# Four-head attention and a graph network on one core: scores by 32-row tiles of TensorE, row sums by VectorE

## The reference

```python
x = _layernorm(x + _L0_gnn_ref(x, adj, ...))   # two graph convolutions, then LSTMs over windows of 1 to 4 nodes
x = _layernorm(x + _L1_gnn_ref(x, W, adj))     # attention, 4 heads of 32 features, masked by adj == 0
x = _layernorm(x + _L2_gnn_ref(x, adj, ...))   # aggregation by the normalized adjacency, two layers, two batch norms
x = _layernorm(x + _L3_gnn_ref(x, W, adj, bias))
```

```python
qkv = h @ W
scores = jnp.einsum("bhid,bhjd->bhij", q, k) / np.sqrt(HEAD_DIM) + mask
attn = jax.nn.softmax(scores, axis=-1)
out = jnp.einsum("bhij,bhjd->bhid", attn, v)
...
agg = jnp.einsum('nm,bmd->bnd', A_hat, features)
h = jax.nn.relu(_batchnorm(x @ W1.T + b1, g1, be1))   # needs the mean and variance over all batches first
```

## Time and profile before

| what | value |
|---|---|
| median of three runs | 1684.76 us (1682.45 to 1689.03) |
| the profiled execution's own time | 1689.47 us |
| its span in the profile | 1687.7 us |
| mean granted TensorE clock | 0.962 |
| busy: PE, DVE, ACT, POOL | 90%, 75%, 62%, 24% |
| stretch of the LSTM block | 0 to 803 us |
| stretch of attention | 803 to 1364 us |
| both later stretches | 1364 to 1688 us |

### The profile page before, as it was taken

How to read it: one execution, slowest core, us unless ns; L and a number is a source line. 1 busy time by engine, 2 the same in 40 slices (tenths; PEclk the granted TensorE clock), 3 DMA queues, 4 the chain that set the end, 5 groups by cost and what they waited for, 6 DMA issues and landing times.

```text
span 1687.7 us, 28097 instructions
## 1 busy us (share of the span) xinstructions
PE 1514.9 (90%) x9014; PEld 1208.4 (72%) x9076; DVE 1263.0 (75%) x2989; ACT 1042.9 (62%) x1984; POOL 407.1 (24%) x641
## 2 busy tenths in 40 slices
PE   3999999899989989995699999999999879899997
PEld 3888888787888888895477767677777645555554
DVE  3578767677776777777688888888888745577775
ACT  2666576566656666664466666666666436557776
POOL 2122212112121221221233233323333300023332
PEclk9999999999999999998799999999999979989999
DMA  3000000000000000000000000000000000022221
GB/s 95 1 1 24 15 1 13 14 13 14 1 26 13 1 13 14 13 1 15 1 20 14 19 12 19 19 12 19 12 19 12 19 19 0 0 70 87 87 87 57
DMA packets 19519, 37.62 MB, mean 22 GB/s; under 512 B 3313, under 2 KB 4849, under 8 KB 19313
## 3 DMA queue, kind: packets, MB, share of 16 engines
q1 hardware_dynamic: 18576, 34.49, 6.4%
q10 hardware_dynamic: 864, 2.11, 0.3%
HBM read 19.81 MB, written 16.78 MB: 22 GB/s over the span
## 4 chain that ended last, share of the span: by engine, by line
PE 61%; DVE 18%; ACT 12%; issue 5%; POOL 2%; DMA 1%; ACTq 0%; DVEq 0%; POOLq 0%
PE banks L391 14%; PE banks L393 13%; PE banks L392 13%; PE banks L1497 5%; PE banks L1504 5%; ACT early_scratch L796 4%; PE banks L1464 3%; DVE x_all L506 3%; ACT attention_scratch L750 2%; ACT attention_rounded L750 2%; PE banks L1414 2%; DVE early_scratch L985 2%; PE banks L1424 2%; DVE consts L464 1%; DVE attention_rounded L1035 1%
## 5 line engine op out<-in xcount | busy, mean ns | idle before, releaser
L391 PE MATMUL banks<-early_rounded 128*128 128x128 f32 (+3 forms) x1424 | 458.4, 322 | 64.9 <-DVE early_rounded L990 31.1
L392 PE MATMUL banks<-early_rounded 128*128 128x128 f32 (+3 forms) x1424 | 454.8, 319 | 0.0
L393 PE MATMUL banks<-early_rounded 128*128 128x128 f32 (+3 forms) x1424 | 454.4, 319 | 0.0
L796 ACT ACTIVATE early_scratch<-banks,consts 128x256 f32<-128x256 f32 (+2 forms) x624 | 311.7, 565 | 133.4 <-PE banks L393 119.3
L391 PEld LDWEIGHTS banks<-early_rounded 128*128 128x128 f32 x1424 | 280.3, 197 | 90.3 <-issue 42.0
L392 PEld LDWEIGHTS banks<-early_rounded 128*128 128x128 f32 x1424 | 280.1, 197 | 14.7
L393 PEld LDWEIGHTS banks<-early_rounded 128*128 128x128 f32 x1424 | 280.2, 197 | 14.0
L660 POOL CAST early_rounded<-early_scratch 128x512 fp32r<-128x512 f32 (+2 forms) x160 | 93.5, 594 | 555.7 <-DVE early_scratch L985 555.7
L750 ACT ACTIVATE attention_rounded<-banks 32x512 fp32r<-32x512 f32 (+1 forms) x160 | 94.4, 590 | 100.3 <-PE banks L1376 69.3
L803 ACT ACTIVATE early_scratch<-early_scratch 128x256 f32<-128x256 f32 (+2 forms) x176 | 87.2, 517 | 71.8 <-DVE early_scratch L976 60.9
L985 DVE TENSOR_TENSOR early_scratch<-early_scratch 128x256 f32<-128x256 f32 (+2 forms) x176 | 96.3, 559 | 42.5 <-ACT early_scratch L803 40.2
(11 more groups left out here) (173 smaller groups left out, 3110.6 us busy)
## 6 DMA issues: line engine op xcount, KB each, us to landing
early_scratch<-in_x_dram SPq DMA_DIRECT2D x16, 512.0 KB, 3.5
x_away<-attention_scratch SPq DMA_DIRECT2D x32, 256.0 KB, 2.0
late_scratch<-x_away SPq DMA_DIRECT2D x32, 256.0 KB, 2.7
out_dram<-late_scratch SPq DMA_DIRECT2D x32, 256.0 KB, 2.0
x_all<-in_WihT_dram ACTq DMA_DIRECT2D x1, 1024.0 KB, 5.5
x_all<-in_WhhT_dram ACTq DMA_DIRECT2D x1, 768.0 KB, 7.2
x_all<-in_Wqkv_dram ACTq DMA_DIRECT2D x1, 192.0 KB, 10.5
kept_scratch<-in_W_dram SPq DMA_DIRECT2D x1, 192.0 KB, 2.5
```

Source lines behind the costliest of these rows:

```text
L391: pe.matmul(out, wt[0], mv[0], start=start, stop=False)
L392: pe.matmul(out, wt[1], mv[0], start=False, stop=False)
L393: return pe.matmul(out, wt[0], mv[1], start=False, stop=stop)
L796: nc.scalar.activation(gate_f[lane][gate][:, 0:cols], bank(bank_set("lstm", n, unit), gate)[:, 0:cols], ACT.Tanh if gate == G else ACT.Sig ...
```

## The change

Scores: q and k are kept as plain float32 (q_f, k_f; one copy each, no low parts, no block-diagonal tiles). A group's scores now fill banks 0 to 3, one bank for each head. After four mask matmuls of 512 columns, 16 matmuls follow (L1402, batch outside, head inside), each with the 32 rows of its head and 128 by 128 columns. The next group's masks wait until both halves of this group's scores are subtracted. `soft` now takes two batches at once, 1024 columns in one instruction, and so does the exponential; there are two parts in place of four.

Sums: vals has 32 columns for a head and no ones. The four heads of `attend` (L1416) go to rows 0, 32, 64 and 96 of one bank, so a group fills one bank, is copied out once and is turned back by four transposes (`back`). The sums of the exponentials are taken by VectorE from the probabilities (`sum`, L1066, two of 1024 columns for a group), inverted (L1070) and multiplied in one instruction (L1075).

Other work moves: the copies of values go from VectorE to ScalarE, the layer norm is applied by ScalarE (four activations with bias and scale, L853) with a shift that GpSimd makes (one product more). The residual is still added by GpSimd, now as `padd`, placed last in its list. The work on the normalized adjacency comes ahead of the lists, and the memsets of the block-diagonal tiles and of the ones are gone. All four lists are new, with up to 6 groups between the first and last step where there were 4, and the table HOME says which bank each step uses: turn, attend and back share 7; keys, values and aggregate 4; queries, first 0 and two of probT 6; the rest 5.

The core of the diff:

```diff
+        HOME = {("aggregate", 0): 4, ("attend", 0): 7, ("attend", 1): 7, ("attend", 2): 7, ("attend", 3): 7,
+                ("back", 0): 7, ("first", 0): 6, ("first", 1): 5, ("keys", 0): 4, ("probT", 0): 5, ("probT", 1): 6,
+                ("probT", 2): 6, ("probT", 3): 5, ("queries", 0): 6, ("turn", 0): 7, ("values", 0): 4}
...
+        fm = Area(mid.enter_context(nc.sbuf_tensor("attention_scratch", [P, 17 * GC], F32)))
...
+        q_f, k_f = fm.take(GC), fm.take(GC)
+        prob = [fm.take(2 * HEADS * P) for _ in range(2)]
...
+        vals = [fm.take(GB * HEADS * DH) for _ in range(2)]
...
                 if what == "rstd":
...
+                    pool.wait_ge(rstd2, g + 1)
+                    _, (_, _, _, mean, _, rstd) = ln_cols(0, GB)
+                    nc.gpsimd.tensor_tensor(shift_cols[:, 0:GB], mean, rstd, ALU.mult).then_inc(shift2, 1)
...
-            groups(pool, [("add", 0, 3), ("rstd", 0, 3), ("copy", 0, 0), ("x2_low", 0, 3)], do, pairs=3)
+            groups(pool, [("rstd", 0, 4), ("copy", 0, 0), ("x2_low", 0, 4), ("padd", 0, 3)], do, pairs=4)
...
-                    for h in range(HEADS):
-                        copy(key_block(kd_r[place][0], h), by_batch(banks[h * DH:(h + 1) * DH, 4, :], GB))\
-                            .then_inc(k_hi, 1)
+                    wait_if(act, scores, g)
+                    copy(k_f, home("keys")).then_inc(k_kept, 1)
...
+                if what == "values":
+                    act.wait_ge(v_sums, g + 1)
+                    wait_if(act, attended, (g - 1) * GB)
+                    copy(vals[place], home("values")).then_inc(v_kept, 1)
                 if what == "exp":
-                    act.wait_ge(shifted, g * GB + part + 1)
+                    act.wait_ge(shifted, g * 2 + part + 1)
                     nc.scalar.activation(prob[part], prob[part], ACT.Exp).then_inc(exps, 1)
...
+                    act.wait_ge(shift2, g + 1)
+                    wait_if(act, x2_lo, g)
+                    wait_if(act, x2_stored, g * 16)
+                    _, (_, _, _, _, _, rstd) = ln_cols(0, GB)
+                    for b in range(GB):
+                        ins = nc.scalar.activation(x2_f[:, b * P:(b + 1) * P], y_f[:, b * P:(b + 1) * P], ACT.Identity,
+                                                   bias=shift_cols[:, b:b + 1], scale=rstd[:, b:b + 1])
...
+            groups(act, [("norm", 0, 4), ("att", 0, 3), ("keys", 0, 1), ("round", 0, 4), ("exp", 0, 2),
+            ("queries", 0, 1), ("values", 0, 1), ("turned", 0, 0), ("probT", 0, 2), ("probT", 1, 2),
+            ("aggregated", 0, 4), ("exp", 1, 2), ("probT", 2, 2), ("probT", 3, 2)], do, pairs=4)
...
+                if what == "sum":
...
+                    nc.vector.tensor_reduce(out=sums[place][:, part * n:(part + 1) * n].rearrange("q (b h) -> q h b", h=HEADS),
+                                            in_=heads_of(prob[part]), axis=AX.X, op=ALU.add).then_inc(summed, 1)
+                if what == "add":
+                    dve.wait_ge(summed, g * 2 + 2)
+                    nc.vector.reciprocal(rden, sums[place]).then_inc(inverted, 1)
...
+                    wait_if(dve, x2_kept, g)
+                    parts = [ap.rearrange("q (n d) -> q n d", d=DH) for ap in (y_f, home("back"))]
+                    nc.vector.tensor_tensor(parts[0], parts[1], rden.unsqueeze(2).broadcast_to([P, GB * HEADS, DH]),
+                                            ALU.mult).then_inc(y_made, 1)
...
+            groups(dve, [("sum", 0, 2), ("stats_of", 0, 5), ("turned", 0, 0), ("agg_low", 0, 4), ("sum", 1, 2),
+            ("soft", 0, 1), ("stats_of", 1, 5), ("add", 0, 2), ("soft", 1, 1), ("stats", 0, 2)], do, pairs=4)
...
+            pe.wait_ge(hat_work_done, 5)
+            pe.wait_ge(ones_made, 1)
+            pe.matmul(banks[:, 0, 0:P], ones_sq, diag, start=True, stop=True).then_inc(hat_product, 1)
...
+            ATTENTION = [("keys", 0, 1), ("attend", 0, 3), ("attend", 1, 3), ("attend", 2, 3), ("attend", 3, 3),
+            ("first", 1, 6), ("queries", 0, 1), ("back", 0, 3), ("values", 0, 1), ("turn", 0, 0),
+            ("probT", 0, 2), ("probT", 1, 2), ("aggregate", 0, 4), ("first", 0, 5), ("scores", 0, 1),
+            ("probT", 2, 2), ("probT", 3, 2)]
+            DRAINED = {"turn": (xT_lo, 1), "keys": (k_kept, 1), "aggregate": (agg_lo, 1), "queries": (q_kept, 1),
+                       "values": (v_kept, 1), "back": (y_made, 1), "probT": (probT_kept, GB), "first": (bn1_done, 2),
+                       "attend": (att_kept, 1)}
...
-                if what == "score":
...
-                    at = part * HEADS * P
-                    pe.matmul(out, ident_bf[:, :], mask[:, :], start=True, stop=False)
-                    mm3(pe, out, cut(q_r, part * P, (part + 1) * P), cut(keys, at, at + HEADS * P), start=False)\
-                        .then_inc(scores, 1)
+                if what == "scores":
+                    if isinstance(g, int) and g == 0:
+                        pe.wait_ge(hat_turned, 1)
+                    wait_if(pe, shifted, g * 2)
+                    for h in range(HEADS):
+                        pe.matmul(banks[:, h, :], ident_bf[:, :], mask[:, :], start=True, stop=False)
+                    pe.wait_ge(k_kept, g + 1)
+                    pe.wait_ge(q_kept, g + 1)
+                    for b in range(GB):
+                        for h in range(HEADS):
+                            rows, cols = slice(h * DH, (h + 1) * DH), slice(b * P, (b + 1) * P)
+                            ins = pe.matmul(banks[:, h, cols], q_f[rows, cols], k_f[rows, cols], start=False,
+                                            stop=b == GB - 1)
+                    ins.then_inc(scores, 1)
...
-                        at, rows = (part * HEADS + h) * VW, (h % 2) * VW
-                        ins = pe.matmul(banks[rows:rows + VW, 6 + h // 2, part * P:(part + 1) * P],
-                                        vals[place][:, at:at + VW], probT[part][:, h * P:(h + 1) * P],
+                        rows, of = slice(h * DH, (h + 1) * DH), (part * HEADS + h) * DH
+                        ins = pe.matmul(banks[rows, HOME[(what, part)], part * P:(part + 1) * P],
+                                        vals[place][:, of:of + DH], probT[part][:, h * P:(h + 1) * P],
                                         start=True, stop=True)
...
+                if what == "back":
+                    pe.wait_ge(att_kept, g + 1)
+                    for b in range(GB):
+                        ins = pe.transpose(home(what)[:, b * P:(b + 1) * P], attT[:, b * P:(b + 1) * P], ident)
                     ins.then_inc(att_turned, 1)
...
+            groups(pe, ATTENTION, do, pairs=4)
```

217 lines of the change are left out of this document (72 added, 145 removed).

## The result

The changed kernel takes 1520.36 us (median of four runs, 1516.75 to 1524.0) for 1686.51 before (1682.45 to 1689.03). The ratio is 0.9017, with an interval of 0.8984 to 0.905. The forecast was 1542, 8.5% faster; measured are 9.8%. The profiled execution took 1516.75 us, with a span of 1515.0.

What follows compares the result with a forecast made beforehand. TensorE, VectorE close behind, was taken to bound attention: 8.9 us untiled plus 1.2 scores and 1.2 attends made 11.3, with 0.9 gaps 12.2 per period; 34 periods plus 3 us led to 1542 us, range 1518 to 1612.

Steps and rivals of the forecast that it cites:

- The bound: Attention before the change: TensorE limits, busy 394.5 of 420 us, VectorE close behind; a group takes 16.5 us.
- Four tiles side by side: Scores and attends: four heads' tiles overlap, 8 steps of 0.107 us, so 1.2 us each per group.
- the way in and out: Entering and leaving tiled work on TensorE: 0.16 us per old attend, 0.3 us added to scores.
- TensorE without the tiles: TensorE's matmuls and transposes outside scores and attends: 8.9 us per group.
- The gaps: TensorE's idle time per period: 2.1 us before, mostly waits for a copy just made; 0.9 us kept after.
- fourth rival: VectorE ends last: TensorE without gaps, VectorE's 11.1 plus 0.3 us, 1515 us; chance counted in the forecast's 0.53.
- The loop: Through y_f, division to next group's division: about 10.4 us, not last; as rival about 13.0, 1569 us, chance 0.12.
- The ends: Attention's stretch outside steady running: 34 periods kept for 32 groups, plus 3 us at the start for adjacency work.
- The range: Whole kernel's time: from 1518 us, near VectorE's bound, to 1612, pairs with 0.5 us more gaps per period.
- Pairs: Rival for scores and attends: tiles overlap only two at a time, 2.0 us each, 1596 us; chance 0.25.
- no overlap: Rival for scores and attends: tiles run one after another, 3.7 us each, 1712 us, slower; chance 0.07.
- The rule on switches: TensorE: switching tiling mode drains the engine; four switches per group for six before, sum left at 11.3 us.

Runs made afterwards that it cites:

- e1: Changed kernel with the scores' 16 matmuls ordered head outside, batch inside: 1574.43 us, ratio 0.9338.
- e3: Changed kernel without VectorE's two sums of exponentials (divided by one instead): 1521.59 us, ratio 0.9025.
- b1: Kernel before the change, leaving out VectorE's four low parts of the keys: 1678.44 us, ratio 0.9954.
- b3: Kernel before the change, with attends as full-width matmuls over pairs of heads instead of column tiles: 1693.35 us, ratio 1.0039.
- e2: Changed kernel without the four mask matmuls of each group (scores unmasked): 1515.5 us, ratio 0.8983.
- e6: Changed kernel with two more GpSimd additions of 512 columns put into the moments: 1537.41 us, ratio 0.9117.
- e10: Changed kernel with the four attends in two pieces, keys between the second and the third: 1530.63 us, ratio 0.9068.
- e5: Changed kernel with another step between every two attends, so four pieces: 1574.62 us, ratio 0.9341.
- e8: Changed kernel with all 16 attend matmuls in one step, head outside, batch inside: 1569.55 us, ratio 0.9297.

## Why the prediction was right, point by point

- **The bound.** TensorE bounds now, shown from both sides: e1 adds 1.65 us to its work and gets 1.65 of period, e3 takes 2.3 us from VectorE and gets nothing. That it bounded before was right only together with its waits: b1 rules VectorE's load out, but b3 makes the attends longer, and the waits gave most of it back.
- **Four tiles side by side.** Right, and read from one row of pairs. Scores were put at 1.2 us and are 1.10, attends at 1.2 and are 1.01. The price for the way in and out was put at 0.3 for each; in the records only the first four are late (214 ns to the next for 111 in the scores, 134 for 109 in the attends). What it costs the neighbours is in the next term.
- **TensorE without the tiles** was 8.9. The rest of the period, 11.40 - 1.10 - 1.01, is 9.29. The 0.4 us are at the changes from one kind of work to another: keys add 0.87 us for 0.69, queries with a half of first 1.49 for 1.38, the other half 0.76 for 0.69, the masks 0.97 for 0.92. By chance this and the two tiled terms, 0.29 too high together, nearly cancel: 11.3 summed, 11.40 measured.
- **The gaps, 0.9 us, were the term that failed.** TensorE is busy for 300.00 of 300 us, and its rows from start to start fill the 11.40, so they are nil. 12.2 - 11.40 is 0.8, and 34 x 0.8 = 27 us of the 30 between 1546.6 and 1516.75 are this. (Between the medians, 1542 and 1520.36, it is 22, since this profiled execution lies below its median and that of before lay above.) The step behind it is the sentence that put the gaps of before down to waits for a copy just made, with VectorE's load as a reason to keep some. b1 shows that VectorE's load made next to none. Nor were most of them waits for a copy just made: 0.9 of the 2.1 us stood at two other waits, and an estimated 0.6 was the price of three pieces of tiles. The new kernel has the attends in one piece, and its lists keep the waits under cover.
- **VectorE** was put at 11.1 us: 288.86 / 300 x 11.40 = 10.98. ScalarE at 10.4: 9.6. GpSimd at 5.9: 5.5. That VectorE's bound is near was right; e2 stands at 11.28 with VectorE at 97%, close to the 11.4 of the fourth rival.
- **The loop** was put at 10.4. The longest through the moments is about 9.9 (e6). It doesn't end last.
- **The ends.** 34 periods and 3 us: 396.4 - 34 x 11.40 = 8.8 us, so 5.8 more than taken. Against that stood, by luck, the 6.3 us by which the LSTM block happened to end earlier, and 2.1 in the stretches behind.
- **The range** went down to 1518, and the period was to lie between 11.4 and 14 us. Both hold only at their edge, the time by 2.4 us and the period, 11.40, by nothing: a period without gaps was the least that was foreseen.
- **The rivals.** Pairs (2.0 us each) and no overlap (3.7) are refuted by the records in fours. The Trainium skill ("TensorE: Matmul & The Clock Gate", Part 1) has 62 ns per matmul where the microcode decodes. Counted for each record, as the prediction did, that isn't what happens here: 32 records in 1.10 us are 34 ns each. Counted for each of the 16 matmuls of the program it would be 0.99 us, and these runs can't tell that from the tiles' own 0.11 us for a four. The fourth rival, 1515 us, which had been counted with the forecast, was nearer to the truth than the forecast, though not by its mechanism.
- **The rule on switches.** The Trainium skill ("TensorEngine Tiling (Array Packing)", Key Properties) has a switch of tiling mode drain the engine. The prediction drew from it that both readings leave the sum alone. e10 gives the price, 0.34 us for one piece more, and by it the order of the attends was worth more than the sum showed: with four pieces (e5) the change would have gained 54 us less, of which 3 x 0.34 x 34 = 35 us are the pieces and the rest is the wait for the copy.

The 5.1 us of a period (16.5 to 11.4) are then: 12 matmuls of 512 columns less, 2.8; four transposes less, 0.4; attends 2.36 to 1.01, 1.35; scores' tiles, 1.10 more; gaps and ways between kinds of work 2.1 to 0.4, 1.7 less. These are counts times rows. No run undoes the row tiles or the new lists alone, so what the lists gave by themselves, a part of the last 1.7, isn't shown. That the tiled terms hang on tiles running side by side is: undoing the scores' order costs 1.65, the attends' 1.54.

## What to carry to other kernels

Small matmuls on different tiles run side by side only if neighbours in the program go to different tiles: put the loop over tiles inside, and keep all tiled work of a stage in one piece. A gap ahead of a tiled matmul holds the switch as well as the wait that the table names: in e10 the last full-width matmul ahead of a piece added 0.32 us for 0.23, in the kernel before 0.53. When the bound is nearly full, look at the second and third limit before cutting further: here 0.97 us less of work gave 0.12. When TensorE and VectorE are both above 95%, the busy shares don't say which one sets the period; take work from each in turn, as e3 did.

## What the runs showed of the hardware

- Four row tiles of 32 rows, or four column tiles of 32 columns, start 7 ns apart, and 128 float32 columns then take 0.11 us for all four: 32 records in 1.10 and 1.01 us.
- With eight records of one tile in a row, a record of the next tile starts about four records ahead (at 554 ns where the first tile's records run from 0 to 884), the same for rows (e1) and for columns (e8, 466 ns).
- One more piece of column tiles costs 0.34 us (e10), of which 0.2 lies in the full-width neighbours. Two column tiles, with eight records for an attend, gained 0.28 us over four attends (b3), almost nothing.
- The scores' tiles start slowly, 214 ns from the first four to the next for 111. A full-width float32 block can do so too: in b3's trace the first record of an attend behind an mm3 is followed after 213 ns in about half of the cases, and behind transposes after 112. So tiles aren't needed for the slow start; what makes it is open.
- The LSTM block ended at 797.1 to 803.8 us in the profiled runs, though the edits don't touch its lists. That alone is 6.8 us of the scatter between kernels; the period is the finer measure, 11.40 us in nearly every group.
